# A two-layer recurrent block on eight cores: the scan's carried state read by heads on two halves of TensorE's rows

## What is computed

```python
xn = _layernorm(x)
s = mamba2(layer_norm(xn))        # below; xn is added to it
g = silu(swiglu(xn, w_gate, w_up, w_down))
x = x + s * g

# mamba2: 8 heads of 256 channels (p), state of 64 numbers (n)
def step(h, inp):                  # one token
    dec_t, dtx_t, B_t, C_t = inp
    h = dec_t[:, :, None, None] * h + dtx_t[..., None] * B_t[:, None, None, :]
    y = jnp.einsum('bhpn,bn->bhp', h, C_t)
    return (h, y)
y = (y + D_skip * xs) * silu(z);  return y @ W_out + b_out
```

## Time and profile before

| | us |
|---|---|
| median of 3 runs | 2907.36 |
| lowest, highest | 2905.17, 3013.18 |
| profiled execution | 2907.51 |
| its span, slowest core (core 1) | 2905.7 |
| spans of the eight cores | 2882.4 to 2905.7 |
| granted clock, mean of each core | 0.985 to 0.993 |

### The profile page before, as it was taken

One profiled execution on the slowest core, in us unless ns is written; L12 is line 12 of the kernel. 1 busy time (PEld: TensorE's weight loads), 2 busy tenths in 40 slices (PEclk: granted clock), 3 DMA queues, 4 the chain that ended last, 5 costly groups with the idle time before them and its releaser, 6 DMA issues.

```text
span 2905.7 us, 42937 instructions; the slowest of 8 cores (2882.4 to 2905.7 us)
## 1 busy us (share of the span) xinstructions
PE 2786.7 (96%) x15702; PEld 1503.3 (52%) x15702; DVE 1633.1 (56%) x2875; ACT 1133.9 (39%) x1686; POOL 566.5 (19%) x987
## 2 busy tenths in 40 slices
PE   2899999999979999999999999999999999999997
PEld 1344444488868874444444444444444444444443
DVE  5845565567787745555544666666666523333333
ACT  4755555866666523334433334333333300000000
POOL 0121121123333333444410221111111110000000
PEclk9999999999999999999999999999999999999999
DMA  8588786578888787787844666545654453334432
GB/s 268 182 268 278 255 270 227 183 197 243 239 260 261 223 223 225 218 215 200 227 133 153 172 167 178 166 145 171 180 164 152 156 143 136 131 137 138 143 137 77
DMA packets 253726, 555.18 MB, mean 191 GB/s; under 512 B 26480, under 2 KB 113360, under 8 KB 251472
## 3 DMA queue, kind: packets, MB, share of 16 engines
q1 hardware_dynamic: 172496, 312.98, 34.1%
q0 software_dynamic: 81024, 239.45, 28.7%
HBM read 382.95 MB, written 201.64 MB: 201 GB/s over the span
## 4 chain that ended last, share of the span: by engine, by line
PE 79%; DMA 9%; DVE 7%; ACT 2%; SPq 2%; issue 1%; POOL 0%; DVEq 0%; POOLq 0%; ACTq 0%
PE ps L397 12%; PE ps L1339 12%; PE ps L1345 11%; PE ps L1468 11%; PE ps L1060 8%; PE ps L1481 7%; PE ps L1041 7%; PE ps L725 5%; DMA gv<-gt 4%; DMA xr<-xT 2%; SPq L101 2%; DVE cl L568 1%; PE ps L1205 1%; PE ps L1211 1%; PE ps L827 1%
## 5 line engine op out<-in xcount | busy, mean ns | idle before, releaser
L397 PE MATMUL ps<-xnT,Lh 128*128 128x512 bf16 x2048 | 459.6, 382 | 8.2 <-ACT hst L401 5.3
L725 PE MATMUL ps<-WW,Hh 128*128 128x256 bf16 x4096 | 454.4, 274 | 8.3 <-DMA WW<-h 8.3
L725 PEld LDWEIGHTS ps<-WW,Hh 128*128 128x128 bf16 x4096 | 402.2, 98 | 57.8 <-issue 9.8
L1468 PE MATMUL ps<-Hh,hl 128*128 128x512 bf16 x1536 | 341.5, 379 | 0.0
L397 PEld LDWEIGHTS ps<-xnT,Lh 128*128 128x128 bf16 x2048 | 200.8, 98 | 243.7 <-issue 19.0
L1347 DVE TENSOR_TENSOR hgs<-sg,ps 128x512 bf16<-128x512 bf16 x192 | 131.5, 685 | 289.9 <-PE ps L1345 145.1
L1342 ACT ACTIVATE sg<-ps 128x512 bf16<-128x512 f32 x192 | 111.2, 596 | 389.7 <-PE ps L1339 375.6
L1468 PEld LDWEIGHTS ps<-Hh,hl 128*128 128x128 bf16 x1536 | 150.3, 98 | 181.2
L401 ACT ACTIVATE hst<-ps,cons 128x512 bf16<-128x512 f32 x256 | 171.9, 687 | 182.1 <-PE ps L397 149.2
L1492 ACT ACTIVATE gx<-ps 128x512 f32<-128x512 f32 x64 | 38.2, 597 | 513.8 <-DVE sx L1494 503.0
L1491 DVE TENSOR_TENSOR sx<-sx,ps 128x512 f32<-128x512 f32 x64 | 44.1, 689 | 340.1 <-PE ps L1481 339.5
(11 more groups left out here) (215 smaller groups left out, 4123.3 us busy)
## 6 DMA issues: line engine op xcount, KB each, us to landing
gt<-thx POOLq DMA_DIRECT2D x64, 512.0 KB, 4.9
h<-hst SPq DMA_DIRECT2D x128, 256.0 KB, 4.5
wst<-W2T POOLq DMA_DIRECT2D x64, 512.0 KB, 6.3
WW<-h SPq DMA_DIRECT2D x16, 2048.0 KB, 14.3
xq<-x1t POOLq DMA_DIRECT2D x128, 256.0 KB, 5.3
hg<-hgs POOLq DMA_DIRECT2D x96, 256.0 KB, 4.7
hl<-hg SPq DMA_DIRECT2D x32, 768.0 KB, 5.1
xt<-x SPq DMA_DIRECT2D x32, 512.0 KB, 9.5
```

The costliest lines, as they stand in the source:

```text
L397: t = PE.do(lambda e, dc=dc: e.matmul(psum[i][:], Lh[(ft // 8) * 8 + dc][:, (ft % 8) * 128:(ft % 8 + 1) * 128], xnT[b % 2][:, dc, :], star ...
L725: t = PE.do(lambda q, f=f, fb=fb, e=e: q.matmul(psum[bk][:, e * 256:(e + 1) * 256], Hh[f][:, fb * 128:(fb + 1) * 128], H[:, f // 4, f % 4, :],
L1468: td = PE.do(lambda e, f=f: e.matmul(psum[bd][:], hl[i][:, f, :], wd[f][:, sl], start=(f == 0), stop=(f == 23)), e_tok[(1, n)], t_wd, pf[b ...
```

## The change

The heads' states are no longer read by one matmul with 128 rows against a moving operand half of zeros. Instead each head has a matmul of its own with 64 rows: head 2j the rows 0 to 63 of `stb` and `Cx`, head 2j+1 the rows 64 to 127, 128 columns each. The two write different PSUM banks, 4 for the even head and 5 for the odd one, so both banks belong to every pair; the two L1211 matmuls follow into the same two banks. `Cx` has no zero part, its memset is gone. The multiply by silu(z) is now one per head, 256 columns, and each releases its bank.

```diff
--- before.py
+++ after.py
@@ -1127,15 +1127,13 @@
         return WB + 4096 * k
     Mx = [at(f"Mx{i}", [128, 8, 128], BF16, hi(24 + i)) for i in range(2)]
 
-    Cx = at("Cx", [128, 4, 2, 128], BF16, hi(26))
+    Cx = at("Cx", [128, 4, 128], BF16, hi(26))
     sct = at("sct", [128, 8, 128], BF16, hi(27))
     eL = at("eL", [128, 4, 128], F32, hi(28))
     stf = [at(f"stf{i}", [128, 512], F32, hi(29 + i)) for i in range(2)]
     stb = at("stb", [128, 1024], BF16, hi(31))
     sg = [at(f"sg{i}", [128, 512], BF16, lo(24) + 1024 * i) for i in range(2)]
     hgs = [at(f"hgs{i}", [128, 4, 2, 128], BF16, lo(25 + i)) for i in range(3)]
-
-    t_cx0 = DVE.do(lambda v: v.memset(Cx[:], 0.0), endB[0])
 
     s_sc = [[P.slot(f"sc{i}_{j}") for j in range(3)] for i in range(2)]
     sc_tok = {}
@@ -1185,7 +1183,7 @@
         for e in range(2):
             ccb = bass.AP(CC[:].tensor, 64 * e * T + c * 128, [[T, 64], [0, 4], [1, 128]])
             t2 = el_free[0] = DVE.do(lambda v, e=e, ccb=ccb: v.tensor_mul(
-                Cx[64 * e:64 * e + 64, :, e, :], eL[64 * e:64 * e + 64], ccb), el_tok[c], cx_free[0], t_cx0)
+                Cx[64 * e:64 * e + 64], eL[64 * e:64 * e + 64], ccb), el_tok[c], cx_free[0], endB[0])
         btb = bass.AP(Btok[:].tensor, c * 64, [[NC * 64, 128], [0, 8], [1, 64]])
         wtb = bass.AP(wsT[g][:].tensor, cc * 8, [[128, 128], [1, 8], [0, 64]])
         t3 = DVE.do(lambda v: v.tensor_mul(Bw[:], btb, wtb), bw_free[0], btk_tok[c // 4])
@@ -1199,30 +1197,31 @@
 
     def d_ypair(c, j):
         i = c % 2
-        bk = 4 + j % 2
         X = xsc[i]
+
         for hf in range(2):
-            PE.do(lambda q, hf=hf: q.matmul(
-                psum[bk][:, hf * 256:(hf + 1) * 256], stb[:, j * 256 + hf * 128:j * 256 + (hf + 1) * 128],
-                Cx[:, j].rearrange("p e t -> p (e t)"), start=True, stop=False),
-                ready[c][1], stb_tok[0], pf[bk], tok=False)
+            for e in range(2):
+                PE.do(lambda q, hf=hf, e=e: q.matmul(
+                    psum[4 + e][:, hf * 128:(hf + 1) * 128],
+                    stb[64 * e:64 * e + 64, j * 256 + hf * 128:j * 256 + (hf + 1) * 128],
+                    Cx[64 * e:64 * e + 64, j, :], start=True, stop=False),
+                    ready[c][1], stb_tok[0], pf[4 + e], tok=False)
             for e in range(2):
                 h = 2 * j + e
                 t = PE.do(lambda q, h=h, hf=hf, e=e: q.matmul(
-                    psum[bk][:, hf * 256 + e * 128:hf * 256 + (e + 1) * 128],
-                    X[:, h * 256 + hf * 128:h * 256 + (hf + 1) * 128], sct[:, h, :], start=False, stop=(e == 1)),
+                    psum[4 + e][:, hf * 128:(hf + 1) * 128],
+                    X[:, h * 256 + hf * 128:h * 256 + (hf + 1) * 128], sct[:, h, :], start=False, stop=True),
                     ready[c][0], sc_tok[c][1], tok=(e == 1 and hf == 1))
-
-        def by_head(a):
-            return a[:, 4 * j:4 * j + 4, :].rearrange("p (e f) t -> p f e t", e=2)
-        pf[bk] = DVE.do(lambda v: v.tensor_mul(
-            by_head(yst[i]), psum[bk].rearrange("p (f e t) -> p f e t", f=2, e=2), by_head(zc[i])),
-            t, sc_tok[c][2], *yst_free[i])
+        for e in range(2):
+            h = 2 * j + e
+            pf[4 + e] = DVE.do(lambda v, e=e, h=h: v.tensor_mul(
+                yst[i][:, 2 * h:2 * h + 2, :], psum[4 + e][:, 0:256].rearrange("p (f t) -> p f t", f=2),
+                zc[i][:, 2 * h:2 * h + 2, :]), t, sc_tok[c][2], *yst_free[i])
         yt[c] = t
         if j == 3:
             cx_free[0] = sct_free[0] = t
-            sc_free[i][2] = (pf[bk],)
-            y_tok[c] = P.dma(POOL, s_y[i], y_d[c], yst[i][:], pf[bk])
+            sc_free[i][2] = (pf[5],)
+            y_tok[c] = P.dma(POOL, s_y[i], y_d[c], yst[i][:], pf[5])
             yst_free[i] = (y_tok[c],)
 
     def d_state(c, q):
```

## The result

The changed kernel takes 2963.85 us (median of 5 runs, 2960.27 to 3113.17) against 2911.65 for the kernel before on the same chips; the ratio is 1.0194 with a 95% interval of 1.0176 to 1.0212. The highest, 3113.17, is from an execution in which the cores of one die ran at a lower granted clock (0.93 to 0.94); the ratio leaves such executions out. The forecast time was 2964.0, the forecast direction slower. The loss is clear of noise, but its interval takes in 2%, on which the prediction had put 0.46 for more and 0.53 for less. The changed kernel's profiled execution took 2966.0 us.

What follows compares the result with a forecast made beforehand. TensorE, busy 749.6 of 752 us in the scan stage, was taken to bound the kernel. Matmuls 37.4 plus bank wait 18.6 gave +56 us on 2907.5, so 2964; own range 2955 to 2972, wider range 2942 to 2979.

Steps and rivals of the forecast that it cites:

- The drain: TensorE, scan stage: 0.095 us lost per shape change; with saved columns, 1.17 us a chunk, 37.4 us in all.
- No drain between halves of the rows and the full array: Rival for TensorE's pairs: shape changes cost nothing, pair 3 still waits, +1.14 us a chunk, 2943 us; chance 10%.
- The overlap: TensorE: two 64-row matmuls on different row halves start 0.005 us apart, not 0.055 as in a row.
- The bank: Before pair 3, TensorE waits for pair 2's late multiply on VectorE: 0.60 us in 31 chunks, 18.6 us.
- Drains, but no wait: Rival at pair 3: shape changes cost as forecast but the second bank is free in time; 2945 us, chance 8%.
- the multiply of 256 columns costs nearly a whole one: Rival on VectorE: pair 3's wait becomes 1.13 us, 16.4 us more in all, 2980 us; chance 10%.
- That the two terms hide each other: Scan stage: pairs 1 and 2 can change cost while the bank's release hardly moves; what pair 3 awaits sets the chunk.
- The memset: Removing memset L1138 (0.91 us) gains 0, as TensorE waits for ScalarE's CC there; bounds 0 to -0.9.

Runs made afterwards that it cites:

- a_mulfirst: Changed kernel with unit f+2's gate/up multiply on VectorE queued behind pair 2's two multiplies of yst; 2944.09 us, ratio 1.0112.
- b_shape: Kernel before, with L1205 reading only the even head's 64 rows, 256 columns, into the same one bank; ratio 1.0163.
- a_grouped: Changed kernel with each pair's four 64-row matmuls together between the two halves' L1211, two shape changes instead of four; 2957.59 us, ratio 1.0162.
- a_grouped_mulfirst: Changed kernel with two shape changes a pair and pair 2's multiplies ahead of unit f+2's; ratio 1.0031.

## Why the prediction was right

It was right in its number and, what the runs add, in its parts. That the median of 2963.85 meets 2964 to a fifth of a microsecond is luck: four of its executions lie between 2960.27 and 2966.01, and the slowest core had a loss in its first chunk that was not in the sum, part of which other stages gave back (below).

- *The drain.* 0.095 us for each change of shape and 0.01 for the first matmul after it, read from two shapes of the kernel before, gave 1.17 us a chunk. With the wait removed (a_mulfirst) the stage grew by 37.2 us, forecast 37.4; b_shape, which has only this term, by 50.1, forecast 50. "No drain between halves of the rows and the full array" is refuted by both. The time is lost in both directions, and whether the matmuls ahead have 128 or 512 columns. The trace is in line with the rule of the Trainium skill, TensorEngine Tiling (Array Packing), Key Properties, that a changed mode drains TensorE, and the page's "up to 2x" for 64 rows (Theoretical Speedup) leaves this price out. The rival named a cause as well, a weight load that can't run ahead. The trace shows that the load doesn't run ahead, but it is held for the 0.09 itself; what holds it no row shows. One term was rounded up: a half adds up to 0.37 in the prediction and was entered as 0.38; with 0.37 the term would have been 35 us. The rows have 0.38 (1881.52 to 1881.90 in the timeline of core 3).
- *The overlap.* The four 64-row matmuls of a pair overlap in twos: the two end 0.23 us after the first start, and one alone has a latency of 0.226 (L1180, 0.23), which leaves no room for 0.055 between them; two full-array matmuls of 128 columns in a row (L1211) end 0.28 after the first start. By the Trainium skill, TensorE: Matmul & The Clock Gate, Part 3, row tiles start about 4 ns apart, and the trace agrees: its starts are 0.003 to 0.004 us apart. The change does what it says: the columns are saved, 0.05 us a half, and the two changes of shape cost four times as much.
- *The bank.* A multiply of a pair is 0.42 us long and the second starts 0.34 after the first, as on the straight line between the 128- and 512-column rows. TensorE resumed 0.14 us after it. 0.60 us a chunk, 18.6 in all, against 18.9 measured by difference. The list of waits alone would have misled: it gives 6.7 us in 28 waits on core 3, for it counts only the idle time ahead of the pair and not the 0.33 between its first two matmuls. The prediction had L1167 still waiting for eL by 0.05 us; the second eL and the multiplies of pair 1 end within 0.02 us of each other, so this slack (0.20 before) was used up. "Drains, but no wait" is refuted by a_mulfirst, "the multiply of 256 columns costs nearly a whole one" by the rows.
- *That the two terms hide each other* was a sentence in the prediction, and a_grouped and a_grouped_mulfirst show its size: the multiply's place is worth 0, 18.9 or 33.7 us, depending on how fast the pairs ahead of it are.
- *The memset* gave nothing that can be seen.
- *What was left out:* the first chunk. I had 31 equal waits. On core 4 the wait in the first chunk is 2.91 us, and the stage there is 810.4 us, 5.5 longer than on core 3 (see below). The slowest core before, core 1, had 748.9. So the slowest cores differ by 61.5 us in this stage and by 58.5 in their spans; the other 3 came back outside it, which no run explains. I had forecast neither, and in the span they partly cancel.

## What to carry to other kernels

Saving columns on TensorE by going to fewer rows is worth its while only if the columns saved between two changes of shape cost more than the changes, so the matmuls of the other shape must stand together: here a change of shape costs as much as 225 columns (0.095 / 0.216 x 512) in each direction, and two changes bracketed a saving of 0.05 us. Before a bank's release becomes a condition, ask when it is released today, not how busy the engine is that releases it: VectorE was 38% idle, and the one multiply that mattered was 1.13 us late behind an instruction that waited for another engine. An instruction that is ready and stands behind one that still waits can be exchanged with it, but that pays only where somebody waits for its result: 0 us in the kernel before, 18.9 in the changed one.

## What was not expected

The wait in the first chunk has a consequence of its own. On core 4 of the changed kernel, TensorE's timeline:

```profile
1594.57 0.59 PE L1204 MATMUL ps<-Cx,stb 64*128 64x128 bf16 x2 [2.91 <-DVE yst L1217]
1595.10 0.40 PE L1211 MATMUL ps<-sct,xsc 128*128 128x128 bf16 x2
...
1599.93 2.43 PE L1344 MATMUL ps<-xg,Hh 128*128 128x512 bf16 x8
```

The stretch of that chunk on core 4 and on core 0 (busy us and instructions of PE, PEld, DVE, ACT and POOL, granted clock, DMA share, GB/s):

```profile
1579.00:1609.00 30.00, 26.75 (x132) 11.53 (x133) 15.06 (x34) 8.95 (x12) 3.10 (x5) 0.89 0.58 193
```

```profile
1565.00:1590.00 25.00, 24.72 (x137) 10.93 (x136) 15.34 (x34) 8.95 (x12) 2.76 (x4) 1.00 0.66 231
```

And on core 4, who waited for whom in that stretch:

```profile
ACT eL L1163 <- DMA Lb<-Lr: 3.1, 1, 3.1
DVE Lb L1167 <- ACT eL L1163: 3.0, 1, 3.0
PE ps L1204 <- DVE yst L1217: 2.9, 1, 2.9
```

After 2.91 us without work TensorE's matmuls are slower for a while: L1211 has 0.40 us for two where it has 0.28, and the eight L1344 have 2.43 where eight take 1.89 elsewhere. The granted clock of the stretch is 0.89, so part of it lies at the lower of the two levels (1.2 GHz against 2.4); on core 0 it stayed at 1.00. The three waits say where the time came from: ScalarE waited 3.1 us for the transfer of Lb before it could begin eL, so the whole chain of the decay was late, and the bank with it. In the kernel before the same transfer was late as well on most cores (1.5 us on core 1), and nothing came of it: the stage was 748.8 to 749.4 us long on every core, and TensorE never waited for yst. The length of the stage on the slowest core of the two kernels:

```profile
L1235 PE MATMUL ps<-xsc,Bw x256: 272/285/297, 1578.1 to 2327.0; 128*64 128x256 bf16 x128
```

```profile
L1234 PE MATMUL ps<-xsc,Bw x256: 272/297/423, 1578.6 to 2389.0; 128*64 128x256 bf16 x128
```

Such a fall isn't tied to the long bank wait alone: in a_mulfirst the same transfer kept ScalarE waiting 4.4 us on core 4, TensorE stood 0.56 us for yst and then 1.18 us for sg in the first chunk, and the granted clock there was 0.94. In the changed kernel cores 1 and 4 show it, and since the metric is the slowest core it can reach the result.
